# Reordering a pair of blocks in an attention kernel: whole value products, earlier second softmax, copies moved across the pair boundary

## What is computed

```python
x = x + _L0_xattn_ref(_layernorm(x), ctx_4096, Wq, bq, Wkv, bkv, Wo, bo)
x = x + _L0_ffn_ref(_layernorm(x), router_w, router_b, A, Bm)
...
q = (query @ Wq + bq).reshape(B, L, NKV, G, HDIM)      # B 32, L 64, NKV 8, G 4, HDIM 128
scores = jnp.einsum('blkgd,bmkd->bkglm', q, k) * scale
attn = jax.nn.softmax(scores, axis=-1)
o = jnp.einsum('bkglm,bmkd->blkgd', attn, v).reshape(B, L, NHEAD * HDIM)
return o @ Wo + bo
```

## Time and profile before

| | |
|---|---|
| median of three runs | 1050.05 us |
| the profiled execution, time / span | 1051.96 / 1050.2 us |
| PE busy | 1031.8 us, 98% |
| DVE, POOL, ACT busy | 802.3, 686.5, 561.5 us |
| chain that ended last | PE 81%, DVE 8%, DMA 4%, POOL 3% |
| granted TensorE clock, mean | 0.991 of 2.4 GHz |
| 14 pairs (277.2 to 961.9 us) | 48.84 us each |

### The profile page before, as it was taken

How to read it: one execution, slowest core, us unless ns; L and a number is a source line. 1 busy time by engine, 2 the same in 40 slices (tenths; PEclk the granted TensorE clock), 3 DMA queues, 4 the chain that set the end, 5 groups by cost and what they waited for, 6 DMA issues and landing times.

```text
span 1050.2 us, 17349 instructions
## 1 busy us (share of the span) xinstructions
PE 1031.8 (98%) x5409; PEld 856.9 (82%) x5409; DVE 802.3 (76%) x1410; ACT 561.5 (53%) x1324; POOL 686.5 (65%) x573
## 2 busy tenths in 40 slices
PE   9999999998999999999999999999999999999997
PEld 7878887877888888888888888888888888887886
DVE  3563455479987987897788879887987797789974
...
GB/s 312 210 130 247 311 215 89 390 349 231 120 262 140 232 166 203 192 168 259 100 295 94 310 100 260 130 239 144 216 220 150 243 116 291 91 140 12 1 1 160
DMA packets 85658, 197.99 MB, mean 189 GB/s; under 512 B 10560, under 2 KB 43368, under 8 KB 70384
## 3 DMA queue, kind: packets, MB, share of 16 engines
...
...
## 4 chain that ended last, share of the span: by engine, by line
PE 81%; DVE 8%; DMA 4%; POOL 3%; ACT 1%; issue 1%; SPq 1%; DVEq 0%; ACTq 0%
PE banks L1738 24%; PE banks L1739 23%; PE banks L1740 23%; PE banks L1890 5%; PE banks L1865 3%; PE banks L1866 3%; DMA k_raw<-keys_dram 2%; PE banks L1765 1%; DVE stats L1278 1%; DVE xo L1203 1%; POOL w_l L629 1%; DMA raw<-in_L_xattn_Wkv_dram 1%; DMA raw<-in_L_xattn_Wq_dram 1%; POOL xo L629 1%; DMA y<-in_ctx_dram 1%
## 5 line engine op out<-in xcount | busy, mean ns | idle before, releaser
L1738 PE MATMUL banks<-wo_h,xo 128*128 128x512 f32 x512 | 204.0, 398 | 0.8 <-DVE y L1681 0.6
L629 POOL TENSOR_TENSOR qT_l<-parts,qT_h 128x512 fp32r<-128x512 f32 x128 | 165.3, 1298 | 58.1 <-ACT qT_h L860 58.0
L1739 PE MATMUL banks<-wo_l,xo 128*128 128x512 f32 x512 | 200.0, 391 | 0.0
L1740 PE MATMUL banks<-wo_h,xo 128*128 128x512 f32 x512 | 199.5, 390 | 0.0
L1738 PE MATMUL banks<-xo,w_h 128*128 128x512 f32 x448 | 176.7, 394 | 1.1 <-DVE parts L1328 1.1
L1739 PE MATMUL banks<-xo,w_h 128*128 128x512 f32 x448 | 174.9, 390 | 0.0
L1740 PE MATMUL banks<-xo,w_l 128*128 128x512 f32 x448 | 174.3, 389 | 0.0
L629 POOL TENSOR_TENSOR xo<-sT,xo 128x512 fp32r<-128x512 f32 (+1 forms) x72 | 102.6, 1425 | 69.2 <-ACT xo L860 69.2
L1203 DVE TENSOR_TENSOR xo<-banks,xo 128x512 fp32r<-128x512 f32 (+1 forms) x156 | 100.8, 665 | 34.4 <-ACT xo L860 33.8
L1738 PEld LDWEIGHTS banks<-wo_h,xo 128*128 128x128 f32 x512 | 96.1, 188 | 24.2 <-DVE y L1681 0.6
L1740 PEld LDWEIGHTS banks<-wo_h,xo 128*128 128x128 f32 x512 | 96.1, 188 | 20.9
...
## 6 DMA issues: line engine op xcount, KB each, us to landing
...
```

What stands on the lines that cost most here:

```text
L629: return nc.gpsimd.tensor_tensor(dst, src, high_part.bitcast(F32), ALU.subtract)
L1738: mm(dst, stat[0], mov[0], start=start, stop=False)
L1739: mm(dst, stat[0], mov[1], start=False, stop=False)
L1740: return mm(dst, stat[1], mov[0], start=False, stop=stop)
```

## The change

The change keeps every operation of the steady pairs and moves many. On PE, the value product of unit 2d-2 goes from behind product 6 to behind product 7; the two chunks of unit 2d-1, which stood apart, come together behind `out` 3, and with them `product(3, 1)` and the second scores go there. The output blocks and the second chunk of that value product get fixed banks:

```diff
 DUO_TASKS = 2 * OPS + 2 * UT
+OUT_SLOTS = (2, 3, 1, 0, 0, 1, 2, 3)
+PV_SLOTS = (2, 3)
...
-def value_place(u, c, i, early=False):
-
-    if early and c == 0:
+def value_place(u, c, i, d=None, k=None):
+
+    if d is not None and k == 0 and c == 0:
         return att[:, i, :]
+    if d is not None and k == 1 and c == 1:
+        return ring[:, PV_SLOTS[i], :]
...
-    return (DUO_TASKS * p + len(PROD) + j) % RING
-
 def opening_duo(d):

     return isinstance(d, int) and d < DUOS

+def product_slot(d, p, k, r):
+
+    return ((DUO_TASKS * p if opening_duo(d) else 0) + PROD_AT[k, r]) % RING
+
+def out_slot(d, p, j):
+
+    return (DUO_TASKS * p + len(PROD) + j) % RING if opening_duo(d) else OUT_SLOTS[j]
```

The waits and the order on PE:

```diff
+        elif (k, r) == (3, 1) and not opening_duo(d):
+            pe.wait_ge(y_added, d * 8 - 8 + 3)
...
+        elif d is not None and k == 1 and c == 1:
+            pe.wait_ge(y_added, d * 8 - 8 + 2)
+        elif d is not None:
             pe.wait_ge(o_low, u * 4)
         elif isinstance(u, int) and u == NU - 2 and c == 1:
...
     def out(d, p, j):

-        if j < 4:
+        if opening_duo(d) and j < 4:
             pe.wait_ge(summed, d * len(SUMS) + SUM_AT[("c22", "c12")[j // 2], j % 2])
+        elif opening_duo(d):
+            pe.wait_ge(y_added, d * 8 - 8 + j - 4 + 1)
+        elif j in (0, 1, 2, 3, 5):
+            name, r = {0: ("c22", 0), 1: ("c22", 1), 2: ("c21", 1), 3: ("c12", 0), 5: ("c12", 1)}[j]
+            pe.wait_ge(summed, d * len(SUMS) + SUM_AT[name, r])
+        elif j == 4:
+            pe.wait_ge(y_added, d * 8 - 8 + 4)
         else:
-            pe.wait_ge(y_added, d * 8 - 8 + j - 4 + 1)
-        out_project(2 * d - 2 + j // UT, out_slot(p, j), j % UT)
+            pe.wait_ge(o_low, (2 * d - 1) * 4 + 3 + j - 6)
+        out_project(2 * d - 2 + j // UT, out_slot(d, p, j), j % UT)

     def opening():

...
         product(g, p, 6, 1)
-        outputs(2 * d - 2, 0, True)
-        outputs(2 * d - 2, 1, True)
         product(g, p, 2, 0)
         product(g, p, 2, 1)
         product(g, p, 7, 0)
         product(g, p, 7, 1)
+        outputs(2 * d - 2, 0, d, 0)
+        outputs(2 * d - 2, 1, d, 0)
         product(g, p, 4, 0)
         product(g, p, 4, 1)
         product(g, p, 5, 0)
...
             pe.wait_ge(wo_low, (STEPS + g) * KC + KC)
         out(d, p, 0)
         scores(d, 0, 0)
-        product(g, p, 3, 1)
         out(d, p, 1)
-        scores(d, 0, 1)
-        outputs(2 * d - 1, 0)
         out(d, p, 2)
         out(d, p, 3)
-        outputs(2 * d - 1, 1)
+        outputs(2 * d - 1, 0, d, 1)
+        outputs(2 * d - 1, 1, d, 1)
+        product(g, p, 3, 1)
+        scores(d, 0, 1)
         out(d, p, 4)
         out(d, p, 5)
         scores(d, 1, 0)
```

VectorE, `duo`:

```diff
         s_peak(2 * d - 1, 0)
         y_sum(d, p, 0)
+        s_add(2 * d - 1, 1)
+        y_sum(d, p, 1)
         s_max(2 * d - 1, 1)
-        y_sum(d, p, 1)
         s_sum(2 * d - 1, 0)
         s_peak(2 * d - 1, 1)
         query_sum(d, p, "c11", 0)
         query_sum(d, p, "c11", 1)
-        output_low(2 * d - 2, 0, 0, True)
-        output_low(2 * d - 2, 0, 1, True)
         s_inverse(2 * d - 1, 0)
         z_sum(g, d, p, 0)
         z_sum(g, d, p, 1)
         s_sum(2 * d - 1, 1)
         query_sum(d, p, "c21", 0)
+        output_low(2 * d - 2, 0, 0, d, 0)
+        output_low(2 * d - 2, 0, 1, d, 0)
         query_sum(d, p, "c21", 1)
-        p_turn(2 * d - 1, 0)
         w_sum(d, p, 0)
         query_sum(d, p, "c22", 0)
+        p_turn(2 * d - 1, 0)
         w_sum(d, p, 1)
-        output_low(2 * d - 2, 1, 0, True)
+        output_low(2 * d - 2, 1, 0, d, 0)
         query_sum(d, p, "c22", 1)
         s_inverse(2 * d - 1, 1)
+        output_low(2 * d - 2, 1, 1, d, 0)
+        query_sum(d, p, "c12", 0)
+        p_turn(2 * d - 1, 1)
         add(0)
-        output_low(2 * d - 2, 1, 1, True)
-        p_turn(2 * d - 1, 1)
-        query_sum(d, p, "c12", 0)
         s_add(2 * d, 0)
-        query_sum(d, p, "c12", 1)
         s_max(2 * d, 0)
         add(1)
+        s_peak(2 * d, 0)
+        add(2)
+        s_sum(2 * d, 0)
+        add(3)
+        s_inverse(2 * d, 0)
+        output_low(2 * d - 1, 0, 0, d, 1)
+        output_low(2 * d - 1, 0, 1, d, 1)
+        p_turn(2 * d, 0)
+        query_sum(d, p, "c12", 1)
+        output_low(2 * d - 1, 1, 0, d, 1)
+        output_low(2 * d - 1, 1, 1, d, 1)
         s_add(2 * d, 1)
-        s_peak(2 * d, 0)
         s_max(2 * d, 1)
-        output_low(2 * d - 1, 0, 0)
-        output_low(2 * d - 1, 0, 1)
-        add(2)
-        s_peak(2 * d, 1)
-        s_sum(2 * d, 0)
         if split:
             combine_w(g + 1, 1, False)
-        output_low(2 * d - 1, 1, 0)
-        add(3)
-        if split:
             combine_w(g + 1, 2, False)
-        s_inverse(2 * d, 0)
-        output_low(2 * d - 1, 1, 1)
+        add(4)
+        s_peak(2 * d, 1)
+        s_add(2 * d + 1, 0)
+        add(5)
         s_sum(2 * d, 1)
-        p_turn(2 * d, 0)
+        add(6)
+        s_inverse(2 * d, 1)
         if split:
             combine_w(g + 1, 3, False)
-        add(4)
-        add(5)
+        if not last:
+            s_max(2 * d + 1, 0)
         if last:
-            ln_stats("f", 0)
-        s_inverse(2 * d, 1)
+            tile_stats("f", 0)
+            add(7)
+        p_turn(2 * d, 1)
+        if last:
+            for t in range(1, 4):
+                tile_stats("f", t)
+            ln_combine("f", 0)
+        else:
+            add(7)
         if split:
             combine_w(g + 1, 4, False)
-        s_add(2 * d + 1, 0)
-        p_turn(2 * d, 1)
-        if not last:
-            add(6)
-            s_max(2 * d + 1, 0)
-            add(7)
-        if not last:
-            s_add(2 * d + 1, 1)


     steps = count(1)
```

ScalarE, `duo` (where it starts and from the query block c22 on; the four `output_high` of unit 2d-2 are also put together ahead of `swap_sum(2d-1, 1)`):

```diff
-        first_product(d, p, 0)
         keys_high(2 * d)
-        first_product(d, p, 1)
         exponents(2 * d - 1, 0)
...
         query_high(d, "c22", 0)
         probs_high(2 * d - 1, 0)
         copy_half(2 * d, 0)
+        query_high(d, "c12", 0)
+        query_high(d, "c22", 1)
+        probs_high(2 * d - 1, 1)
+        swap_max(2 * d, 0)
         if split:
             split_q(g + 1, [0], False)
-        probs_high(2 * d - 1, 1)
-        query_high(d, "c12", 0)
+        exponents(2 * d, 0)
+        swap_sum(2 * d, 0)
+        output_high(2 * d - 1, 0, 0, d, 1)
+        output_high(2 * d - 1, 0, 1, d, 1)
+        output_high(2 * d - 1, 1, 0, d, 1)
+        output_high(2 * d - 1, 1, 1, d, 1)
+        probs_high(2 * d, 0)
+        copy_half(2 * d, 1)
+        keys_high(2 * d + 1)
         query_high(d, "c12", 1)
-        copy_half(2 * d, 1)
-        swap_max(2 * d, 0)
-        query_high(d, "c22", 1)
-        output_high(2 * d - 1, 0, 0)
-        output_high(2 * d - 1, 0, 1)
         swap_max(2 * d, 1)
-        exponents(2 * d, 0)
-        keys_high(2 * d + 1)
-        output_high(2 * d - 1, 1, 0)
-        output_high(2 * d - 1, 1, 1)
-        swap_sum(2 * d, 0)
-        exponents(2 * d, 1)
+        copy_half(2 * d + 1, 0)
         if split:
             split_q(g + 1, [2], False)
+        exponents(2 * d, 1)
+        swap_sum(2 * d, 1)
         values_high(2 * d)
-        swap_sum(2 * d, 1)
-        probs_high(2 * d, 0)
-        copy_half(2 * d + 1, 0)
         if split:
-            split_q(g + 1, [1, 3, 5, 4, 6], False)
+            split_q(g + 1, [1], False)
+        if not last:
+            swap_max(2 * d + 1, 0)
         probs_high(2 * d, 1)
         if not last:
+            first_product(d + 1, 1 - p, 0)
+        if split:
+            split_q(g + 1, [3], False)
+        if not last:
+            first_product(d + 1, 1 - p, 1)
             copy_half(2 * d + 1, 1)
-        if not last:
-            swap_max(2 * d + 1, 0)
+        if split:
+            split_q(g + 1, [5, 4, 6], False)

     for name in START:
         n = pos.get(name)
```

GpSimd, `duo`, from the query block c22 on:

```diff
         query_low(d, "c22", 0)
+        shift(2 * d, 0)
         query_low(d, "c12", 0)
         query_low(d, "c22", 1)
-        shift(2 * d, 0)
-        query_low(d, "c12", 1)
-        keys_low(2 * d + 1)
-        shift(2 * d, 1)
-        normalise(2 * d, 0)
         if split:
             split_q(g + 1, [0], False)
+        normalise(2 * d, 0)
+        probs_low(2 * d, 0)
+        keys_low(2 * d + 1)
+        query_low(d, "c12", 1)
+        shift(2 * d, 1)
+        if split:
+            split_q(g + 1, [2], False)
         values_low(2 * d)
-        probs_low(2 * d, 0)
+        if split:
+            split_q(g + 1, [1], False)
         normalise(2 * d, 1)
-        if split:
-            split_q(g + 1, [2, 1], False)
         probs_low(2 * d, 1)
         if split:
-            split_q(g + 1, [3], False)
+            split_q(g + 1, [3, 5], False)
         if p == 1 and last_group:
             root("f", 0)
         shift(2 * d + 1, 0)
         if split:
-            split_q(g + 1, [5, 4, 6], False)
+            split_q(g + 1, [4, 6], False)
     split_wo(0, range(KC))
     root("x", 8)
     root("x", 12)
```

65 lines of the change are left out of this document (33 added, 32 removed), and 2 rows, old and new, of the table VECTOR_TAIL.

## The result

| | before | after |
|---|---|---|
| median | 1048.69 us (4 runs, 1046.2 to 1051.24) | 1067.60 us (4 runs, 1065.73 to 1070.59) |
| ratio | | 1.0183, 95% interval 1.0161 to 1.0206 |
| profiled execution, time / span | 1051.96 / 1050.2 us | 1070.59 / 1068.8 us |
| mean granted clock | 0.991 | 0.986 |

The change makes the kernel 1.8% slower, well over three times the half per cent that a measurement of this kernel can tell from no change. The forecast was slower, at 1058.0 us, and the time lies above the range (1044.5 to 1064).

The account below looks back on a forecast made before the run. TensorE's matmul stream was taken to bound the kernel (98% busy, no waits in the pairs); -5.7 (stream) + 9.6 (handovers) + 4.0 (tail) = +7.9 us, giving 1058.0 us against the 1050.05 median; range 1044.5 to 1064.

Parts of the forecast that it names:

- the saving in the stream: PE's matmuls in the fourteen pairs: two value product entries instead of three, 0.41 us a pair, -5.7 us (4.5 to 6.5).
- the entry cost is none: Rival: gaps around value products belong to something else, forecast rises by up to 5.7 us; 0.06 together with every pair stops.
- the tail: Behind the last pair: late second value product and first output block, +4.0 us, between 2 and 4.5.
- nearly fits: Rival: PE stops 0.1 to 0.5 us per second pair, tail loses 2 to 4; 1049.4 us (1046 to 1055), chance 0.32.
- no new wait: Rival: VectorE keeps its old lead and only the shorter stream shows, 1044.4 us; chance 0.15.
- every pair stops: Rival: c12 row 1 or output block 0 late in all 14 pairs, +10, 1068 us; 0.06 together with the entry cost rival.
- the handover from first to second pair: 0.8 us left at output block 0, 0.5 to 0.9 at scores(d, 1, 0); costed at nothing.
- the handover, the second term of the sum: Second pairs of groups 1 to 6 handing over to the next group: 6 x 1.6 = +9.6 us (+0.6 to +17).
- The first stop: At product(6, 1), waiting for add(7): 11.05 us against PE's 10.5, so PE stops for 0.55 us.
- the walk of VectorE from `add(7)` to c22: Next group's start: 13.45 us of steps plus 3.0 of holds, 16.45 against PE's 15.45; 1.0 us lost.
- `s_inverse` meet a whole GpSimd instruction more: High end of the handover: 1.25 us more each, 2.85 us a pair, +17 us in all.
- the walk to the first output block: In the tail: output_low starts 6.2 us after the last pair's end instead of 1.8, first output block 4.4 us later.

Follow-up runs that it names:

- e10: Changed kernel with GpSimd's last two weight parts of a second pair computed on 64 of 512 columns, a timing probe; 1061.53 us, ratio 1.0121.
- e2: Changed kernel with VectorE's s_inverse(2d-1, 0) behind the two z_sum instead of ahead of them; 1058.90 us, ratio 1.0095.
- e8: Changed kernel with VectorE's copy of the next group's biases ahead of combine_w 3 in the pair before; 1069.23 us, ratio 1.0168.
- e11: e8 with GpSimd's last two weight parts of a second pair also computed on 64 of 512 columns; 1058.14 us, ratio 1.0092.
- e1: Changed kernel with ScalarE's values_high(2d) and high part of weight 1 ahead of swap_sum(2d, 1); 1059.12 us, ratio 1.0093.

## Why the prediction was right and wrong

**Right: the saving in the stream.** The text had 48.42 us for a pair without stops; it is 48.40. Scores are never ahead of a value product any more. Fourteen pairs give -6.2 us against -5.7 forecast, inside the 4.5 to 6.5. The rival that the entry cost is none is out.

**Right: the mechanism and the places of the loss.** PE stops in each of the six handovers and in no other pair but pair 2, at `product(6, 1)` for an add and at output block 0 for `parts`, and at both places named in the tail. The rivals "nearly fits" and "no new wait" are out, and so is "every pair stops": the handover from first to second pair, whose cover the text called thin, holds (48.40).

**Wrong: the handover, the second term of the sum, 1.6 us where 2.81 were measured.** Over the six that is 7.1 of the 10.7 us between the +7.9 forecast and the +18.6 measured. The first stop was sized well: 0.38 and a restart of 0.11, against 0.55. The step that failed is the walk of VectorE from `add(7)` to c22, 16.45 us, measured 17.65 (381.75 to 399.40). PE's own part, 15.45 us, was right: in the pair without stops it takes 15.44. The pieces of the walk: the copy of the biases 1.26 and its wait 0.17 instead of 0.35 for both; the second `s_peak` 0.50 with its wait instead of 1.4, because it came just as the weight parts ended; `s_inverse` 0.91 + 1.18 + 0.25 instead of 1.3. The text had the last at hand ("`s_inverse` meet a whole GpSimd instruction more"), costed 2.85 for it, nearly the 2.81 measured, and took the middle "since its terms are those that the rows show at the same steps". But the edit had moved `s_inverse` to a place where GpSimd's `query_low` starts just ahead of it: its input is ScalarE's copy, right ahead of the swap that `s_inverse` waits for. In the changed kernel GpSimd, still busy, started it 0.16 us before `s_inverse`, in e10, with GpSimd free, 0.82 us before; it was the neighbour both times, so the hold was no matter of chance, only its length was; e2, which takes the whole step out of the way, gains 1.30 us, and e10, which shortens the hold by 0.67 us, gains 0.69. The second fault is of kind: the walk was made for VectorE alone, with holds added as if independent. e8 and e11 show two chains, VectorE's and GpSimd's, that end together. Shortening one gives nothing; a hold on a step that would have waited anyway costs nothing. The restarts of 0.11 us were in no term either, but of the four in a pair only the last adds to it: output block 0 waits for VectorE's sum whatever the first three cost. It starts 22.22 us after the pair instead of 19.55, 2.67 late, and the restart behind it is most of what is left to 2.81.

The rule of the Trainium skill that the prediction weighed (SBUF — State Buffer, "SBUF: two separate sides": the engine that starts first gets the shared ports for its whole instruction, and the other one is blocked) was applied only to `values_low`, as 0.8 us in all that the sum left out. At that step the trace shows 1.46 us, so 0.17 over the 1.29 usual, neither the 0.46 of the sum nor the 0.6 by the rule. The trace agrees with the rule at the small steps of VectorE: three of them (1.26, 1.09 and 1.18 us for some 0.2 of work) end within 0.05 us of the GpSimd instruction that ran. It was weighed at the wrong instruction.

**Wrong: the tail, 5.75 us where 4.0 were taken.** The walk to the first output block said 4.4 us later; 7.75 us after the last pair's end against 3.25 before (965.22 to 961.97) is 4.5. The stop at the second value product said about 2 us, and 2.25 were idle; the first value product was late too (0.48), which the text did not have. Missing from the sum is the halved clock, 2.2 us in one output block. Up to the second output block that makes 14.14 us against 8.01, 6.1 more; 0.4 of it is given back by the end, in a last stretch that ran partly at 1.2 GHz in both profiles.

**Not in the sum:** 0.7 us in pair 2, whose output block 0 waits for `parts` too, and 1.6 us ahead of the pairs. Of the latter, chance is the likely cause: the first query product began at 199.81 and 199.68 in the two profiles of the kernel before, at 200.99 in the changed kernel and at 199.61 in e8_bias_early, whose code is the same up to there; the half clock in the opening is missing in e2_inverse_late, which has the changed kernel's opening.

What stays open: whether moving the last two weight parts of GpSimd behind the second `s_peak` would bring the handover to zero without e1. It was not tried; e10 and e11 only made them shorter.
